# Carried keys and values by head on 64 array columns, values in plain fp32

## The reference, cut to what matters

```
def step_k(hk, x):
    hk = hk * g_t[:, :, None, :] + k_t[..., None] * p_t[:, :, None, :]
    return (hk, jnp.einsum('bhk,bhkm->bhm', q_t, hk))
pvT = jax.nn.softmax(okT, axis=-1)
def step_v(hv, x):
    hv = hv * g_t[..., None] + p_t[..., None] * v_t[:, :, None, :]
    return (hv, jnp.einsum('bhm,bhmv->bhv', pv_t, hv))
```

## Time and profile before

| what | us |
|---|---|
| median of 3 runs (lowest to highest) | 1313.72 (1313.54 to 1313.87) |
| the profiled execution, its own time | 1313.55 |
| its span in the trace | 1311.8 |
| PE busy | 1302.4 (99%) |
| PE weight loads busy | 1150.9 (88%) |
| DVE busy | 934.9 (71%) |
| ACT busy | 535.4 (41%) |
| POOL busy | 425.9 (32%) |

### The profile page before, as it was taken

The page is one execution under the profiler, slowest core; times in us unless marked ns, Lnnn a source line. Parts: engine busy times, 40 slices in busy tenths (PEclk is TensorE's granted clock), DMA queues, the critical chain, the costliest instruction groups (busy, mean ns, idle before and its releaser), DMA issues.

```text
span 1311.8 us, 21997 instructions
## 1 busy us (share of the span) xinstructions
PE 1302.4 (99%) x8652; PEld 1150.9 (88%) x8652; DVE 934.9 (71%) x1887; ACT 535.4 (41%) x1551; POOL 425.9 (32%) x390
## 2 busy tenths in 40 slices
PE   8999999999999999999999999999999999999998
PEld 7888888888888888888888988888888888988886
DVE  5777777777777777777777777777777777766654
ACT  5634443344334443444335434444334434632221
POOL 3412342254223431234125422343133413442211
PEclk9999999999999999999999999999999999999999
DMA  6002100010000100010001000010000110000000
GB/s 232 33 33 81 33 17 1 1 55 10 10 1 25 33 17 1 25 33 17 1 1 49 9 17 1 24 33 17 1 24 26 65 34 1 1 0 33 33 32 33
DMA packets 33847, 36.04 MB, mean 27 GB/s; under 512 B 3536, under 2 KB 24016, under 8 KB 33744
## 3 DMA queue, kind: packets, MB, share of 16 engines
q1 hardware_dynamic: 33744, 34.64, 8.3%
HBM read 30.43 MB, written 4.19 MB: 26 GB/s over the span
## 4 chain that ended last, share of the span: by engine, by line
PE 98%; DVE 0%; DMA 0%; issue 0%; ACT 0%; SPq 0%; POOLq 0%; POOL 0%; DVEq 0%
PE p L1062 15%; PE p L1063 15%; PE p L1064 15%; PE t L1120 5%; PE o L1304 3%; PE s L1188 3%; PE xb L1257 3%; PE p L1188 2%; PE o L1242 2%; PE o L1240 2%; PE t L1304 2%; PE s L1131 2%; PE s L1613 2%; PE s L1132 2%; PE s L1133 2%; PE s L1615 2%
## 5 line engine op out<-in xcount | busy, mean ns | idle before, releaser
L1062 PE MATMUL p<-wvg_hi,xt_hi 128*128 128x512 f32 x508 | 201.5, 397 | 0.0
L1063 PE MATMUL p<-wvg_lo,xt_hi 128*128 128x512 f32 x508 | 198.5, 391 | 0.0
L1064 PE MATMUL p<-wvg_hi,xt_lo 128*128 128x512 f32 x508 | 197.9, 390 | 0.0
L558 POOL TENSOR_TENSOR orstd<-ovar,minus_half 128x8 f32<-128x8 f32 x32 | 52.4, 1638 | 424.4 <-DVE ovar L1013 424.4
L520 POOL TENSOR_TENSOR s_lo<-sums,s_hi 128x512 fp32r<-128x512 f32 x64 | 83.1, 1299 | 225.5 <-ACT s_hi L649 225.5
L1062 PE MATMUL p<-xt_hi,wsqk_hi 128*128 128x512 f32 x372 | 147.9, 397 | 0.0
L1063 PE MATMUL p<-xt_lo,wsqk_hi 128*128 128x512 f32 x372 | 145.4, 391 | 0.0
L1064 PE MATMUL p<-xt_hi,wsqk_lo 128*128 128x512 f32 x372 | 145.1, 390 | 0.0
L624 ACT ACTIVATE v_tok<-p 128x256 f32<-128x256 f32 x128 | 49.6, 388 | 220.2 <-PE p L1064 216.3
L911 DVE COPY hv<-xb 64x128 f32<-64x128 f32 x192 | 55.1, 287 | 88.9 <-PE xb L1257 87.6
L1064 PEld LDWEIGHTS p<-wvg_hi,xt_lo 128*128 128x128 f32 x508 | 95.4, 188 | 20.7
(11 more groups left out here) (284 smaller groups left out, 3555.4 us busy)
## 6 DMA issues: line engine op xcount, KB each, us to landing
raw<-in_L_attn_Wv SPq DMA_DIRECT2D x32, 128.0 KB, 2.3
raw<-in_L_attn_Wg SPq DMA_DIRECT2D x32, 128.0 KB, 2.9
raw<-in_L_attn_Wo SPq DMA_DIRECT2D x16, 256.0 KB, 3.0
acc<-in_L_attn_hidden_states SPq DMA_DIRECT2D x4, 1024.0 KB, 5.6
out<-acc SPq DMA_DIRECT2D x16, 256.0 KB, 2.0
acc<-in_turned SPq DMA_DIRECT2D x3, 1024.0 KB, 8.6
raw<-in_L_attn_Ws SPq DMA_DIRECT2D x8, 256.0 KB, 2.8
raw<-in_L_attn_Wq SPq DMA_DIRECT2D x8, 256.0 KB, 3.0
```

The costliest lines, as they stand in the source:

```text
L558: nc.gpsimd.tensor_tensor(orstd[:], ovar[:], minus_half[:], ALU.pow).then_inc(orstd_done, 1)
L1062: nc.tensor.matmul(out_, lh, rh, start=(k == 0), stop=False)
L1063: nc.tensor.matmul(out_, lh, rl, start=False, stop=False)
L1064: last = nc.tensor.matmul(out_, ll, rh, start=False, stop=(k == n - 1))
```

## The change

The state over keys is made by head: two products, each with 64 array columns (the keys of one head) and 64 moving columns (its slots). The state over values too: two products, each with 64 array columns (the slots of one head) and 128 moving columns, in fp32 as it is. The first head's result goes to partitions 0 to 63 of `XB`, the second's to 64 to 127, and so the first head takes array columns 0 to 63 and the second 64 to 127. The halves `e_tok_hi`, `e_tok_lo`, `v_hi`, `v_lo` and what makes them on ACT and POOL go. `XB` is zeroed once at the start, because the blocks between different heads are no longer written. `hv` becomes 128 by 256 for each chunk, and the copy out of `XB` moves from DVE (two of 64 by 128) to ACT (one of 128 by 256). On PE `running_values` of chunks 0, 1 and 2 move: the first to ahead of the second turn of `y`, the second to behind the slot outputs, the third to behind the turn of `pz`; `running_keys(2)` waits until `hv` of chunk 0 has been copied.

```
@@ attention: tensors, semaphores
-        e_tok_hi = sb("e_tok_hi", [P, CH - 1, P], F32R)
-        e_tok_lo = sb("e_tok_lo", [P, CH - 1, P], F32R)
-            v_hi = early.enter_context(nc.sbuf_tensor("v_hi", [P, CH - 1, VW], F32R))
-            v_lo = early.enter_context(nc.sbuf_tensor("v_lo", [P, CH - 1, VW], F32R))
+        hv = sb("hv", [P, CH - 1, VW])
-        hv = sb("hv", [P, CH - 1, DV])
+        xb_zeroed = sem("xb_zeroed")
@@ cell_gpsimd
                 sums_low(pool, cell.shifted(-1), 0)
+                sums_low(pool, cell.shifted(-1), 1)
-            pool.wait_ge(e_tok_hi_done, cell.count(1, 1))
...
-            for c in range(CH - 1):
-                if c == 1 and not first(cell):
-                    sums_low(pool, cell.shifted(-1), 1)
-                pool.wait_ge(v_hi_done, cell.count(CH - 1, c + 1))
-                nc.gpsimd.tensor_tensor(v_lo[:, c, :], v_tok[:, c, :], v_hi[:, c, :].bitcast(F32),
-                                        ALU.subtract).then_inc(v_lo_done, 1)
@@ scalar
-        def values_high(act, cell, c):
-        def slots_high(act):
+        def keep_values(act, cell, c):
+            act.wait_ge(hv_summed, cell.count(CH - 1, c + 1))
+            nc.scalar.activation(hv[:, c, :], XB[:, P:P + VW], ACT.Copy).then_inc(hv_kept, 1)
@@ cell_scalar
             if not first(cell):
                 y_high(act, cell, 0)
+            keep_values(act, cell, 0)
+            if not first(cell):
                 y_high(act, cell, 1)
                 sums_high(act, cell, 0)
-                act.wait_ge(ok_summed, cell.count(1, 1))
-                slots_high(act)
-                values_high(act, cell, 0)
-            values_high(act, cell, 1)
+            keep_values(act, cell, 1)
...
             values_scalar(act, cell, 2)
-            values_high(act, cell, 2)
             values_scalar(act, cell, 3)
             act.wait_ge(pz_turned, cell.count(1, 1))
             nc.scalar.activation(pz_t[:], PZ_BANK[:], ACT.Copy).then_inc(pz_t_done, 1)
+            keep_values(act, cell, 2)
@@ cell_vector
-            keep_values(0)
...
-            keep_values(1)
...
-                keep_values(2)
@@ vector_part
             nc.vector.memset(own[:], 0.0).then_inc(own_done, 1)
+            nc.vector.memset(XB[:], 0.0).then_inc(xb_zeroed, 1)
@@ cell_tensor, running_keys
                 if c > 0:
                     pe.wait_ge(hk_kept, cell.count(CH - 1, c))
-                nc.tensor.matmul(XB[:, 0:P], k_tok[:, c, :], e_tok[:, c, 1:3, :].rearrange("p h m -> p (h m)"),
-                                 start=(c == 0), stop=True, skip_group_check=True).then_inc(hk_summed, 1)
+                elif first(cell):
+                    pe.wait_ge(xb_zeroed, 1)
+                for h in range(2):
+                    mm = nc.tensor.matmul(XB[h * DK:(h + 1) * DK, h * M:(h + 1) * M], k_tok[:, c, h * DK:(h + 1) * DK],
+                                          e_tok[:, c, 1 + h, :], start=(c == 0), stop=True, skip_group_check=True)
+                mm.then_inc(hk_summed, 1)
+
+            def running_values(c):
+                pe.wait_ge(v_done, cell.count(CH, c + 1))
+                pe.wait_ge(hk_kept, cell.count(CH - 1, min(c + 2, CH - 1)))
+                if c > 0:
+                    pe.wait_ge(hv_kept, cell.count(CH - 1, c))
+                for h in range(2):
+                    mm = nc.tensor.matmul(XB[h * M:(h + 1) * M, P + h * DV:P + (h + 1) * DV], e_tok[:, c, 1 + h, :],
+                                          v_tok[:, c, h * DV:(h + 1) * DV], start=False, stop=True, skip_group_check=True)
+                mm.then_inc(hv_summed, 1)
@@ the loop over chunks of the slot outputs
             for c in range(CH):
+                if c == 2:
+                    running_values(0)
                 if c == 2 and not first(cell):
                     pe.wait_ge(rz_tok_done, cell.count(1, 1))
                     turned_y(pe, cell, 1)
                 if c == 2:
+                    pe.wait_ge(hv_kept, cell.count(CH - 1, 1))
                     running_keys(2)
...
             mm.then_inc(ok_summed, 1)
+            running_values(1)
             if not first(cell):
                 rows_first(pe, cell)
-            def running_values(c):
...
-                parts = ((e_tok_hi, v_hi), (e_tok_hi, v_lo), (e_tok_lo, v_hi))
...
             token_proj(pe, cell, 2)
-            running_values(0)
...
             token_proj(pe, cell, 3)
-            running_values(1)
...
             turned(PZ_BANK, [pz[:, c, :, :].rearrange("p h m -> p (h m)") for c in range(CH)], pz_turned)
+            running_values(2)
             if not last:
                 feature_proj(pe, nxt, 0, s_proj)
-                running_values(2)
@@ L1295
-                                     hv[rows_own, c - 1, :], start=(c == 1), stop=True, skip_group_check=True)
+                                     hv[rows_own, c - 1, h * DV:(h + 1) * DV], start=(c == 1), stop=True, skip_group_check=True)
```

More of the change, by code:

```diff
@@ L304, in attention @@
         th = sb("th", [P, 2, VW])
-        e_tok_hi = sb("e_tok_hi", [P, CH - 1, P], F32R)
-        e_tok_lo = sb("e_tok_lo", [P, CH - 1, P], F32R)
-        with ExitStack() as early:
-            v_hi = early.enter_context(nc.sbuf_tensor("v_hi", [P, CH - 1, VW], F32R))
-            v_lo = early.enter_context(nc.sbuf_tensor("v_lo", [P, CH - 1, VW], F32R))
+        hv = sb("hv", [P, CH - 1, VW])
         y = sb("y", [P, CH, 2, DV])
@@ L393, in attention @@
         pz_t_done = sem("pz_t_done")
-        e_tok_hi_done, e_tok_lo_done = sem("e_tok_hi_done"), sem("e_tok_lo_done")
-        v_hi_done, v_lo_done = sem("v_hi_done"), sem("v_lo_done")
         osq_done, ovar_done, orstd_done = sem("osq_done"), sem("ovar_done"), sem("orstd_done")
@@ L531, in cell_gpsimd @@
                 sums_low(pool, cell.shifted(-1), 0)
-            pool.wait_ge(e_tok_hi_done, cell.count(1, 1))
-            nc.gpsimd.tensor_tensor(e_tok_lo[:].rearrange("p c (h m) -> p c h m", h=2), e_tok[:, 0:CH - 1, 1:3, :],
-                                    e_tok_hi[:].rearrange("p c (h m) -> p c h m", h=2).bitcast(F32),
-                                    ALU.subtract).then_inc(e_tok_lo_done, 1)
-            for c in range(CH - 1):
-                if c == 1 and not first(cell):
-                    sums_low(pool, cell.shifted(-1), 1)
-                pool.wait_ge(v_hi_done, cell.count(CH - 1, c + 1))
-                nc.gpsimd.tensor_tensor(v_lo[:, c, :], v_tok[:, c, :], v_hi[:, c, :].bitcast(F32),
-                                        ALU.subtract).then_inc(v_lo_done, 1)
+                sums_low(pool, cell.shifted(-1), 1)
             if last:
@@ L629, in values_scalar @@
                                  scale=0.5).then_inc(th_done, 1)
-        def values_high(act, cell, c):
-            act.wait_ge(v_done, cell.count(CH, c + 1))
-            nc.scalar.activation(v_hi[:, c, :], v_tok[:, c, :], ACT.Copy).then_inc(v_hi_done, 1)
-        def slots_high(act):
-            nc.scalar.activation(e_tok_hi[:].rearrange("p c (h m) -> p c h m", h=2), e_tok[:, 0:CH - 1, 1:3, :],
-                                 ACT.Copy).then_inc(e_tok_hi_done, 1)
+        def keep_values(act, cell, c):
+            act.wait_ge(hv_summed, cell.count(CH - 1, c + 1))
+            nc.scalar.activation(hv[:, c, :], XB[:, P:P + VW], ACT.Copy).then_inc(hv_kept, 1)
         def y_high(act, cell, half):
@@ L675, in cell_scalar @@
                     car.prep_high(act, n)
-            if first(cell):
-                act.wait_ge(e_tok_done, 1)
-                slots_high(act)
-                values_high(act, cell, 0)
             values_scalar(act, cell, 1)
@@ L905, in cell_vector @@
                 y_vector(dve, cell.shifted(-1))
[L907 to L912, removed]
             def keep_keys(c):
@@ L982, in cell_vector @@
                 car.norm1_tile(dve, 0, 1)
-            if first(cell):
-                slots_vector(dve, nxt)
-                keep_values(2)
[L987 to L990, removed]
             if last:
                 car.x_low(dve, 0, 0, X1[0])
-            elif not first(cell):
+            else:
                 slots_vector(dve, nxt)
```

## The result

The changed kernel takes 1365.9 us (median of 4, 1365.78 to 1366.03) against 1313.8 (1313.54 to 1313.92): ratio 1.0396, 95% interval 1.0383 to 1.0409. It is slower by 52.1 us; the forecast was 1363, slower by 49.9. The profiled execution took 1366.03, with a span of 1364.1.

What follows compares the result with a forecast made beforehand. PE, 99% busy, was taken to bound the kernel. Over 32 cells, 0.99 us of added products plus 2.28 of shape changes less 1.71 removed gives +49.9 on 1313.55, taken as 1363 us; range 1348 to 1386.

Steps and rivals of the forecast that it cites:

- What bounds the kernel: PE, busy 99% of the span; other engines' work moves the time only if it makes PE wait.
- Products side by side: The two heads' column-half products run together: 0.11 us per key piece, 0.22 per value piece, 0.99 a cell.
- second and third rivals: Heads run one behind the other: with shape changes paid, 1395 us, chance 0.10; without them, about 1330, chance 0.07.
- The rule on loads: A PE weight load overlaps running matmuls only where row groups differ, which would hold the second head back.
- Changes of shape: Six visits a cell to column halves on PE, each 0.38 us in and out: 2.28 a cell, 73.0 in all.
- the lower bound: A visit at 0.30 us, both ends at 0.15, as a shorter 64-column load may lower the entry; 57.6 in all.
- The wait for `hv` of chunk 0: Before running_keys(2), PE waits for ACT's copy: free under shape changes, otherwise 0.30 us a cell, 9.6 in all.
- What costs nothing: DVE and POOL savings, ACT copies, zeroing XB and dropped or later-placed waits leave PE's time unchanged: 0 us.
- Sum: Over 32 cells, added products 0.99 plus shape changes 2.28 less removed products 1.71: +49.9 us, giving 1363.
- The first rival: Column halves on PE need no change of shape; 1300 us, faster, chance 0.25; wins under 0.12 us a visit.

Runs made afterwards that it cites:

- e2: Changed kernel with the same column-half products in four visits a cell, not six, keys and values of chunks 0 and 1 standing together: 1344.34 us, ratio 1.0234.
- e1: Changed kernel with only the shape undone, keys and values each one fp32 product on the whole array: 1344.96 us, ratio 1.0239.
- e3: Changed kernel with the second y_sums on DVE moved ahead of add_m24(0) and the reduction of top: 1354.0 us, ratio 1.031.
- e10: Kernel before with all values in one column-half visit behind the transposes of pz, second y_sums directly behind y_low(1): 1309.05 us, ratio 0.9962.
- e9: Kernel before with all values in one column-half visit ahead of head_blocks, reciprocal halved, second y_sums directly behind y_low(1): 1303.68 us, ratio 0.9922.
- e5: Changed kernel with running_values(2) moved directly ahead of head_blocks (64 array rows), ACT's third copy behind keys_scalar: 1359.45 us, ratio 1.0349.
- e8: Kernel before with all values in one column-half visit ahead of head_blocks, reciprocal halved, second y_sums ahead of top: 1311.52 us, ratio 0.9984.

## Why the prediction was right, and where its sizes were off

*What bounds the kernel.* Right: PE's work and what makes it wait; 59 us less on DVE and 111 less on POOL moved nothing.

*Products side by side.* Right: 0.22 for the values behind the keys in e2. The second and third rivals, one head behind the other, fall with it. The rule on loads from TensorE: Matmul & The Clock Gate (Trainium skill, Part 3), by which the second head would have been held back for sharing its rows, is not what these traces show.

*Changes of shape.* The mechanism was right, the term too large: I took 0.38 a visit, 2.28 a cell, and the chain has 0.34 (3.02 - 0.99 = 2.03 a cell). The entry is 0.155 and not 0.20, the effect of the shorter load that I had kept for the lower bound only. Over 32 cells the term was 8.0 us too high.

*The wait for `hv` of chunk 0.* Right in both halves: hidden by the changes of shape in the changed kernel, 0.31 a cell for a predicted 0.30 when they go (e1). In the changed kernel the load behind it starts at 656.65, 0.52 after the end of `running_values(0)` at 656.13, as forecast.

*What costs nothing.* This is the step that failed: "the later-placed waits for the halves are gone, but PE did not wait there". I asked who waits for work that is removed or moved, and not what a moved piece had covered. `running_values(0)`, 0.35 us of PE, stood ahead of `rows_second`, which waits for POOL's `s_lo`, and the 0.18 in place of 0.12 for its first product was there in the trace before as a sign that this wait was already at its limit. "PE did not wait there" was itself not quite so: it waited 2.3 us. The price of the lost cover is 10.6 us (12.9 less 2.3); removing the whole wait gained 11.9 (e3).

*Sum.* 41.9 of visits and products and 10.6 of added waiting make 52.5, for 52.1 measured; the forecast's 49.9 came from one term 8.0 too high and one of 10.6 missing. That it came within 2.2 us is luck, since the two errors nearly cancel. The direction and the range did not need it: with either error alone mended the sum is 41.9 or 60.5, about 1355 or 1374, and both lie within 1348 to 1386. The first rival, no price for the shape, would have needed under 0.12 us a visit; it was 0.34.

## What to carry to other kernels

Count how often a piece of work on part of the array stands alone between work on all of it: each change of shape, in any direction, cost 0.15 to 0.20 us here, nearly as much as a whole product of 128 fp32 columns (0.22). Small products on half the columns paid here only where several stood together (e10), and more so next to another part-array group (e9). When a piece is moved off PE's list, look at what the instruction behind its old place waits for; the cover that it gave is part of its price. Where the first product behind a wait takes longer on the chain than its like, that wait is already at its limit, even where the list of waits says nothing.

## What the runs showed of the hardware that I had not expected

Going from 64 columns to 64 rows is one change and not two (e5, 6.4 us; e9 against e10, 5.4 us). POOL's subtraction of 128 by 512 took 1.30 us beside a DVE operation that reads PSUM and 1.74 us beside DVE's subtraction on `ok` in e8, 0.44 more, where the wait on `s_lo` was 0.27 a cell. The order seems to matter: in e9 POOL's subtraction starts first (625.19) and keeps its 1.29, while DVE's on `ok`, started at 626.20, takes 0.83 instead of 0.69. Why the two hold each other up is not isolated by a run here.
